# Expert layers of a graph network: the first layer's output computed transposed, four steps deep instead of six

## The reference, cut to what matters

```python
def _moe(tokens, router_w, w1, b1, w2, b2):
    logits = tokens @ router_w.T
    probs = softmax(logits)
    rw, re = top_k(probs, 2)
    rw = rw / max(rw.sum(-1), 1e-12)
    combine = zeros((N, 8)).at[arange(N)[:, None], re].set(rw)
    out = tokens
    for e in range(8):
        h = gelu(tokens @ w1[e] + b1[e])      # w1[e], w2[e]: 256 x 256
        y = h @ w2[e] + b2[e]
        out = out + combine[:, e:e + 1] * y
    return out
```

## Time and profile before

| | us |
|---|---|
| median of three runs | 2656.83 (2654.34 to 2657.34) |
| the profiled execution | 2656.25 |
| its span in the profile | 2654.4 |

### The profile page before, as it was taken

The page is one execution under the profiler, slowest core; times in us unless marked ns, Lnnn a source line. Parts: engine busy times, 40 slices in busy tenths (PEclk is TensorE's granted clock), DMA queues, the critical chain, the costliest instruction groups (busy, mean ns, idle before and its releaser), DMA issues. The chain is left out here.

```text
span 2654.4 us, 61287 instructions
## 1 busy us (share of the span) xinstructions
PE 2380.0 (90%) x15214; PEld 2044.3 (77%) x15215; DVE 2007.8 (76%) x6154; ACT 1716.5 (65%) x5986; POOL 1353.1 (51%) x1342
## 2 busy tenths in 40 slices
PE   4399999789999999999999999999999889119997
PEld 4288887568888888888888888888888779117886
DVE  8999999477777777777777777777777656546653
ACT  1777777567777777777777777777777556233432
POOL 2067777465555555555555555555555101267666
PEclk7599999989999999999999999999999989559998
DMA  7011111243232323232322332323235299156675
GB/s 151 1 34 29 34 34 29 86 114 91 87 92 87 91 87 91 87 91 87 91 87 89 89 91 87 91 87 91 87 91 86 62 289 307 67 204 203 208 123 65
DMA packets 155377, 265.16 MB, mean 100 GB/s; under 512 B 31249, under 2 KB 99440, under 8 KB 154917
## 3 DMA queue, kind: packets, MB, share of 16 engines
q0 software_dynamic: 64656, 147.39, 21.2%
q1 hardware_dynamic: 90623, 116.59, 14.6%
HBM read 190.85 MB, written 73.02 MB: 99 GB/s over the span
## 5 line engine op out<-in xcount | busy, mean ns | idle before, releaser
L1056 POOL DMA_INDIRECT work<-dst_half,stage_i x848 | 811.6, 957 | 758.3 <-PE ps L1264 582.5
L1247 PE MATMUL ps<-W2c,work 128*128 128x256 f32 x3392 | 802.3, 379 | 0.0
L1247 PEld LDWEIGHTS ps<-W2c,work 128*128 128x128 f32 x3392 | 612.0, 190 | 70.7
L1082 DVE TENSOR_TENSOR agg<-agg,ps 125x256 f32 x848 | 354.2, 418 | 254.0 <-PE ps L1264 246.3
L1188 ACT ACTIVATE work<-ps 128x512 f32<-128x512 f32 x424 | 251.9, 594 | 351.5 <-PE ps L1264 351.4
L1264 PE MATMUL ps<-work 128*125 128x256 f32 x1696 | 435.2, 379 | 1.3 <-ACT work L1209 1.3
L1203 ACT ACTIVATE work<-work 128x256 f32<-128x256 f32 x848 | 341.4, 404 | 53.6 <-DVE work L1109 50.1
L1161 DVE SCALAR_TENSOR_TENSOR work<-ps,work,b2c 128x256 f32<-128x256 f32 x848 | 368.4, 476 | 0.0
L1238 PE MATMUL ps<-ablk,work 128*128 x2544 | 351.1, 275 | 16.3 <-DVE work L1130 10.4
L519 POOL DMA_INDIRECT edge_records<-stage,work x208 | 262.6, 1263 | 176.2 <-PE ps L946 113.2
L1195 ACT ACTIVATE work<-work 128x256 f32<-128x256 f32 x848 | 340.8, 406 | 0.3
(11 more groups left out here) (280 smaller groups left out, 3366.8 us busy)
## 6 DMA issues: line engine op xcount, KB each, us to landing
work<-tile_sources SPq DMA_DIRECT2D x106, 250.0 KB
first_choice_tokens<-work SPq DMA_DIRECT2D x14, 1028.0 KB
work<-dst_half,stage_i POOLq DMA_INDIRECT x848, 2.8
second_choice_tokens<-work SPq DMA_DIRECT2D x14, 516.0 KB
work<-first_choice_tokens SPq DMA_DIRECT2D x28, 258.0 KB, 3.7
work<-second_choice_tokens SPq DMA_DIRECT2D x28, 258.0 KB, 2.9
work<-first_choice_tokens SPq DMA_DIRECT2D x28, 256.0 KB, 3.4
update_node_half<-work SPq DMA_DIRECT2D x25, 250.0 KB, 2.2
```

The lines of the kernel that those rows point to most:

```text
L1056: pool.indirect_dma_start(bg[:, r, u, :], None, dstd, bass.IndirectOffsetOnAxis(ap=stage_i[:, c:c + 1], axis=0)).then_inc(gath[r], 16)
L1082: v.tensor_tensor(d, d, ps[0:NB, (7, 0)[a.mod(2)], u * D:(u + 1) * D], ALU.add).then_inc(agg_add, 1)
L1247: last = t_.matmul(ps[:, 5 + s, u * D:(u + 1) * D], sT[:, a.mod(RT), u, k], W2c[:, k], start=(k == 0), stop=(k == KC - 1))
```

## The change

The first layer is computed with the expert's weights as the stationary operand and the transposed tokens moving, so that h comes out transposed already and the transposes of h, with ScalarE's copy of them, go. Its stationary operand is read from a fixed place: VectorE copies the two experts' `w1` of a pair to `w1p`, two pairs deep. The bias now lies along partitions, so ScalarE adds it inside the Gelu, in four activations of 128 columns per pair, and reads experts' offsets from registers of its own. `b1` is loaded as 8 rows and transposed by TensorE in the update stage instead of being broadcast by a DMA. The pipeline is four steps deep instead of six; y has four PSUM banks. The wait for `tabrow` moves from SyncE to the engines that read it.

```diff
--- before.py
+++ after.py
@@ -1293,6 +1293,7 @@
         b2b = wcut(X * D)
         rws = wcut(KC * X, "p (k e) -> p k e", k=KC)
         rwr = wcut(D)
+        b1r = wcut(D)
         ub1T = wcut(KC)
         lg = wcut(BK * X, "p (t e) -> p t e", t=BK)
         pr = wcut(BK * X, "p (t e) -> p t e", t=BK)
@@ -1353,6 +1354,7 @@
         aggcp_ready = sem("aggcp_ready")
         rw_tr = sem("rw_tr")
         rwT_ready = sem("rwT_ready")
+        b1T_ready = sem("b1T_ready")
         tb_ready = sem("tb_ready")
         tb_tr = sem("tb_tr")
         tT_ready = sem("tT_ready")
@@ -1372,11 +1374,11 @@
                 sp.dma_start(uW2s, uW2.rearrange("(k p) n -> p k n", p=P)).then_inc(uw_in, 16)
                 sp.dma_start(ub1T, ub1.rearrange("(k p) -> p k", p=P)).then_inc(uw_in, 16)
                 sp.dma_start(rwr[0:X], router_w).then_inc(uw_in, 16)
+                sp.dma_start(b1r[0:X], b1).then_inc(uw_in, 16)
                 expert_weights = [(w1s[:, 0], w1[:, 0:P, :].rearrange("e p n -> p e n")),
                                   (w1s[:, 1], w1[:, P:2 * P, :].rearrange("e p n -> p e n")),
                                   (w2s[:, 0], w2[:, 0:P, :].rearrange("e p n -> p e n")),
                                   (w2s[:, 1], w2[:, P:2 * P, :].rearrange("e p n -> p e n")),
-                                  (b1b, b1.rearrange("e n -> (e n)").partition_broadcast(P)),
                                   (b2b, b2.rearrange("e n -> (e n)").partition_broadcast(P))]
                 WAT = 2
 
@@ -1409,7 +1411,7 @@
                     step(Step(0, RP, m))
                 for n in range(NP2, 2 * UNITS):
                     empty_slots(n)
-                sp.wait_ge(fw_in, 16 * (2 * KC + 2))
+                sp.wait_ge(fw_in, 16 * (2 * KC + 1))
                 sp.wait_ge(xpads_out, 16 * (2 * UNITS + 1))
 
             @block.gpsimd
@@ -1486,9 +1488,11 @@
 
             @block.scalar
             def _(act):
-                act.wait_ge(uw_in, 64)
+                act.wait_ge(uw_in, 80)
                 act.wait_ge(rw_tr, 1)
                 nc.scalar.activation(rws, ps[:, 7, 0:KC * X].rearrange("p (k e) -> p k e", k=KC), ACT.Copy).then_inc(rwT_ready, 1)
+                nc.scalar.activation(b1b.rearrange("p (e n) -> p e n", e=X)[:, :, 0:KC],
+                                     ps[:, 7, KC * X:2 * KC * X].rearrange("p (k e) -> p e k", k=KC), ACT.Copy).then_inc(b1T_ready, 1)
 
                 def step(m):
                     if m.within(NP2):
@@ -1532,9 +1536,11 @@
             @block.tensor
             def _(pe):
                 t_ = nc.tensor
-                pe.wait_ge(uw_in, 64)
+                pe.wait_ge(uw_in, 80)
                 for k in range(KC):
-                    last = t_.transpose(ps[:, 7, k * X:(k + 1) * X], rwr[0:X, k * P:(k + 1) * P], ident[0:X, 0:X])
+                    t_.transpose(ps[:, 7, k * X:(k + 1) * X], rwr[0:X, k * P:(k + 1) * P], ident[0:X, 0:X])
+                for k in range(KC):
+                    last = t_.transpose(ps[:, 7, (KC + k) * X:(KC + k + 1) * X], b1r[0:X, k * P:(k + 1) * P], ident[0:X, 0:X])
                 last.then_inc(rw_tr, 1)
                 pe.wait_ge(rwT_ready, 1)
 
@@ -1648,7 +1654,6 @@
                 sp.wait_ge(xtab_out, 16)
                 sp.dma_start(tabrow[0:1, PADT:PADT + P],
                              xtabd.rearrange("p k -> (p k)").rearrange("(a n) -> a n", a=1)).then_inc(xtab_in, 16)
-                sp.wait_ge(xtab_in, 16)
 
             @block.vector
             def _(dve):
@@ -1741,8 +1746,8 @@
         XP = XT // 2
         XPC = XC // 2
         RX, RY, RS, RH = 8, 4, 4, 4
-        RB = 2
-        LXT, L1, LG1, L2H, LHT, L2 = 1, 2, 3, 4, 5, 6
+        RB, RW = 2, 2
+        LXT, L1, LG1, L2 = 1, 2, 3, 4
         LY = L2 + 1
         LB = RX + 2
         cut(0, restart=True)
@@ -1753,9 +1758,8 @@
         yb = cut(RY * 2 * D, "p (r u n) -> p r u n", r=RY, u=2)
         base = cut(RB * 2 * D, "p (r u n) -> p r u n", r=RB, u=2)
         xsT = cut(RH * 2 * D, "p (r n) -> p r n", r=RH)
-        hg = cut(RH * 2 * D, "p (r u n) -> p r u n", r=RH, u=2)
         hT = cut(RH * 2 * D, "p (r n) -> p r n", r=RH)
-        hb = work[:, WORK - 2 * 2 * D:WORK].rearrange("p (r u n) -> p r u n", r=2, u=2)
+        w1p = cut(RW * 2 * KC * D, "p (r u k n) -> p r u k n", r=RW, u=2, k=KC)
         w1f = w1s.rearrange("p k e n -> p k (e n)")
         w2f = w2s.rearrange("p k e n -> p k (e n)")
 
@@ -1768,10 +1772,8 @@
         xs_tr = sem("xs_tr")
         xsT_ready = sem("xsT_ready")
         slot_row = sem("slot_row")
+        w1p_ready = sem("pair_weights")
         h_ps = sem("h_ps")
-        hb_ready = sem("hb_ready")
-        hg_ready = sem("hg_ready")
-        h_tr = sem("h_tr")
         hT_ready = sem("hT_ready")
         y_ps = sem("y_ps")
         y_raw = sem("y_raw")
@@ -1853,6 +1855,7 @@
                 for t in range(BK):
                     route(t)
 
+                dve.wait_ge(xtab_in, 16)
                 regs = [v.alloc_register(f"expert_of_tile{j}") for j in range(2 * (RX + L2))]
                 offs = [None] * (2 * (RX + L2))
 
@@ -1869,14 +1872,6 @@
                         enter(m // RX)
                     for i in beside(m):
                         route(i)
-                    a = m - L1
-                    if 0 <= a < XP:
-                        dve.wait_ge(h_ps, a + 1)
-                        wait(dve, hg_ready, a - 1)
-                        for u in range(2):
-                            o = offs[2 * (b + L2 - L1) + u]
-                            last = v.tensor_tensor(hb[:, a % 2, u], ps[:, 2 + a % 2, u * D:(u + 1) * D], b1b[:, bass.ds(o, D)], ALU.add)
-                        last.then_inc(hb_ready, 1)
                     a = m - L2
                     if 0 <= a < XP:
                         r = a % RY
@@ -1884,7 +1879,7 @@
                         wait(dve, y_out[r], 32 * (a // RY))
                         for u in range(2):
                             o = offs[2 * b + u]
-                            v.tensor_tensor(yb[:, r, u], ps[:, 6 + a % 2, u * D:(u + 1) * D], b2b[:, bass.ds(o, D)], ALU.add).then_inc(y_raw, 1)
+                            v.tensor_tensor(yb[:, r, u], ps[:, 4 + a % RH, u * D:(u + 1) * D], b2b[:, bass.ds(o, D)], ALU.add).then_inc(y_raw, 1)
                         if a < XPC:
                             dve.wait_ge(base_in[a % RB], 16 * (a // RB + 1))
                         for u in range(2):
@@ -1897,6 +1892,10 @@
                         last.then_inc(yb_ready, 1)
                     a = m - LXT
                     if 0 <= a < XP:
+                        wait(dve, h_ps, a - RW + 1)
+                        for u in range(2):
+                            o = offs[2 * (b + L2 - LXT) + u]
+                            v.tensor_copy(w1p[:, a % RW, u], w1f[:, :, bass.ds(o, D)]).then_inc(w1p_ready, 1)
                         r = a % RX
                         dve.wait_ge(xs_in[r], 16 * (a // RX + 1))
                         if a >= RX:
@@ -1914,7 +1913,19 @@
                     nc.scalar.activation(ts[n_, r, XW:XB], agg[n_, t, :], ACT.Identity, bias=mv3[n_, t:t + 1, 0],
                                          scale=xscale[n_, t:t + 1]).then_inc(base_ready, 1)
 
+                act.wait_ge(xtab_in, 16)
+                regs = [nc.scalar.alloc_register(f"expert_of_tile{j}") for j in range(2 * (RX + LG1))]
+                offs = [None] * (2 * (RX + LG1))
+
+                def enter(it):
+
+                    for j in range(2 * LG1):
+                        nc.scalar.reg_mov(regs[j], 0 if isinstance(it, int) and it == 0 else regs[2 * RX + j])
+                    nc.scalar.load(regs[2 * LG1:], tabrow[0:1, bass.ds(it * (2 * RX) + PADT, 2 * RX)])
+                    offs[:] = [nc.scalar.snap(r, min_val=0, max_val=(X - 1) * D) for r in regs]
+
                 def step(m):
+                    b = m.c % RX if isinstance(m.it, int) else m.c - RX
                     a = m - LXT
                     if a.within(XP):
                         act.wait_ge(xs_tr, a.of(1, 1))
@@ -1922,19 +1933,21 @@
                         nc.scalar.activation(xsT[:, a.mod(RH)], ps[:, a.mod(2), :], ACT.Copy).then_inc(xsT_ready, 1)
                     a = m - LG1
                     if a.within(XP):
-                        act.wait_ge(hb_ready, a.of(1, 1))
-                        wait(act, h_tr, a.of(1, 1 - RH))
-                        nc.scalar.activation(hg[:, a.mod(RH)], hb[:, a.mod(2)], ACT.Gelu).then_inc(hg_ready, 1)
-                    a = m - LHT
-                    if a.within(XP):
-                        act.wait_ge(h_tr, a.of(1, 1))
+                        act.wait_ge(h_ps, a.of(1, 1))
                         wait(act, y_ps, a.of(1, 1 - RH))
-                        nc.scalar.activation(hT[:, a.mod(RH)], ps[:, 4 + a.mod(2), :], ACT.Copy).then_inc(hT_ready, 1)
-                pipeline(act, XP, L2, RX, step)
+                        for u in range(2):
+                            o = offs[2 * b + u]
```

(33 more changed lines are left out.)

## The result

The changed kernel takes 2761.74 us (2759.66 to 2763.84, 4 runs) against 2655.93 (2654.34 to 2657.34, 4 runs) in the same session: ratio 1.0396, 95% interval 1.0383 to 1.0408, some 106 us slower. The profiled execution took 2761.4 with a span of 2759.6. The prediction was 2770, range 2732 to 2832.

What follows compares the result with a forecast made beforehand. TensorE alone bounded the kernel before; the change was to make it alternate with VectorE's copies. The stage's path to 2747.8, less 3 and 2.5 at the start, plus 25 for the clock, gave 2767, so 2770 us; range 2732 to 2832.

Steps and rivals of the forecast that it cites:

- The closed ring: Last stage: second layer, y on VectorE, two copies, first layer run in turn; 6.32 then 6.05 us a pair against 4.33.
- The ring's terms: Parts of one pair's round: 0.15 to y, 1.19 or 1.46 to copies, copies 0.76, 0.24 to TensorE, layers 1.82 and 1.89.
- 2C: VectorE's two weight copies of a pair together, taken as 0.76 us, bounds 0.76 and 1.25.
- The copy: One 128x512 f32 copy within SBUF on VectorE: 0.42 us, or about 0.65 at the 400-element row's pace.
- Start: Last stage begins earlier: -3 us from SyncE not waiting for the tile table, -2.5 from the update stage.
- The update stage: Dropping the 1 MB broadcast of b1 saves 0 to 3.5 us there, taken as 2.5.
- y(0): Start of pair 0's adds on VectorE, moved from step 6 to 4: at 2399.05 in the old time.
- Clock: TensorE's clock falls in the gaps of 2.1 to 2.3 us: 25 us lost, between 0 and 48.
- the rival that took the rule for this case, 2745: Rival: the same alternation of TensorE and VectorE at full clock, 2745 us; chance 0.25.
- End: After pair 53's adds: gate work 1.28, GpSimd 0.27 later, last pairs' writes 3.72 + 3.72 + 3.4, then 8.1 us.
- The rival without a ring, 2635: Rival: copies ready before TensorE ends the second layer, only its 3.99 us a pair counts; 2635 us, chance 0.05.
- GpSimd has no say before: Before the last pairs, GpSimd's 5.1 us while routing and 3.7 later stay under 6 and do not set the pace.

Runs made afterwards that it cites:

- g1: Changed kernel with VectorE's two weight copies moved ahead of y in its step, nothing else: 2660.5 us, ratio 1.0012 to the kernel before.
- a5: Changed kernel with the copies still behind y but made one step ahead, for pair m instead of m-1: ratio 1.002 to the kernel before.
- g2: Changed kernel with each pair's weight copies made twice, the added ones into a spare buffer: 2808.7 us, ratio 1.0563 to the kernel before.
- c1: Changed kernel with the copies ahead of y and the base loads issued two pairs earlier: 2641.2 us, ratio 0.9938 to the kernel before.
- r1: The changed kernel measured again, unaltered, in another session on a second chip: 2762.3 us, ratio 1.0396 to the kernel before.
- g3: Changed kernel with each pair's token transposes done four times over, filling TensorE's gap: 2747.3 us, ratio 1.0338 to the kernel before.

## Why the prediction was right, and by how much each term was off

- *The closed ring* was the mechanism. Shown by its waits in 56 of 56 pairs, by g1 and a5, which open it in two ways and bring back nearly all, and by g2, in which a ring without a fall of the clock is longer by just the copies' time.
- *The ring's terms.* Second layer to y 0.15, y 1.19 (first half 1.46 to 1.50) and 2C = 0.76 (0.80 in some pairs) came out as written. VectorE's end to TensorE's start took 0.05, not the 0.24 of the earlier trace rows; that row is at the lower clock, but so is the first layer at 2458.09, and it starts 0.05 behind its copies as well, so what made 0.24 there stays open. The first layer took 1.89 after an idle gap, not 1.82; without one, in c1, 1.79 (2480.23 - 2478.44). Rings without a fall of the clock took 5.93 to 6.00 and 6.20 to 6.30, on average 5.95 and 6.23, for 6.05 and 6.32: 28 x 6.23 + 25 x 5.95 = 323.2 for 328.2, 5 us too much.
- *The copy.* 426 ns, taken as 420; the bound of 1.25 for two was far off. The Trainium skill, VectorE: DVE Perf Modes, section on the perf-mode tier table, gave an estimated 430 by it; the trace agrees. The 400-element copy of the earlier trace rows at 520 ns does not follow it.
- *Start.* GpSimd's memset came at 2297.68 for 2301.18: 3.5 us earlier, where 5.5 were forecast. From the table's load to the memset are now 0.7 us, which were 3.6, so the wait gave its 2.9 (forecast 3). The update stage gave about 1.4 of the 2.5: its first steps come every 6.2 us now and no longer jump, but they are still late (2152.90, 2159.21, 2165.44, 2170.54), and the table's way out and back took 7.3 us where it had taken 6.5 (2289.64 to 2296.95; before 2291.06 to 2297.55). In the experiments' traces on the two faster chips this memset comes anywhere from 2295.2 to 2300.4, so a term of 1 us here is less than that scatter. y(0) came at 2396.1, 2.6 later than forecast (2399.05 - 5.5).
- *Clock.* 343.1 us between y(0) and y(53), less 323.2 of rings, leave 19.9, where 25 were taken from bounds of 0 and 48. It is a dozen falls of 0.9 to 1.6 us on a first layer (16.8 together) and some 0.3 on the second layer behind each; in r1 ten falls leave 16.4. g3 got 15 of it back. The 25 was a guess between two rows, and that it came within 5 us is in part luck; its kind, a loss per fall of some 1.7, was right, and the frequency (about every third ring up to 2601, none from there to 2727, where most of the gaps are 1.7 instead of 2.0) wasn't to be had from the trace of before. The Trainium skill, TensorE: Matmul & The Clock Gate, section "Loop structure matters more than you think", says that a copy beside the matmuls doesn't bring the clock down, of a loop whose next matmuls follow at once. Here they do not, and the clock fell twelve times; the rival that took the rule for this case, 2745, is what g3 measures (2747) once TensorE works through most of the gap, and not what the kernel does with the gap open.
- *End.* From y(53) to the end 20.3, forecast 20.5. Gelus: four in 1.14, forecast 1.1, never in TensorE's waits. Sum of the differences: 2.6 - 5.0 - 5.1 - 0.2 = -7.7, from 2767.3 to the span of 2759.6. So rings and clock, both taken too long, made nearly all of the miss.
- *The rival without a ring, 2635.* c1 is that kernel: 2641.2, and 220.0 us between y(0) and y(53). Two things were missing from its sum: the base loads, which the ring had covered (49.7 us of waits on VectorE in g1, 19 us of time between g1 and c1), and GpSimd's 5.25 us a step while rows are routed, which the copies hand on to TensorE. (The rival's own sum has a slip: 117 - 110 is 7, not 6.) "GpSimd has no say before: 5.1 us, under 6" was right for the changed kernel and wrong for this rival.

## What to carry to other kernels

When an engine is given a new job for a partner, look at what stands ahead of it in that engine's program order: if that waits for the partner's last output, the two engines run in turns, however many buffers lie between, and the price is the sum of both parts in each round (here 5.9 to 6.3 us for 3.95). Cover is only good for the pace at which it was worked out: once a ring opens, work out each former cover again with the shorter step (here base loads, then GpSimd's writes). And a regular standstill of a matrix engine can cost more than its length, so price it, or give it work.

## What the runs showed of the hardware

- With standstills of 2.0 to 2.1 us in rounds of about 6 us the granted clock fell in about every third round (0.91 over 2400 to 2577), and the 16 matmuls behind took 3.2 to 3.7 us for 2.05. With 1.7 to 1.8 us it fell in none of the rounds of the changed kernel from 2605 to 2722. With mostly 0.4 to 0.8 us, the rest filled with transposes (g3), it stayed at 1.00 from 2400 to 2700.
- Sixteen 128 x 128 f32 products, a new weight each, take 1.79 us back to back (c1), as against 1.73 for the eight of 256 columns that they replace: here twice the weight loads cost 0.06 us in 1.73.
- One edit gave 0.9973 on one chip and 1.0012 on another, with intervals that don't touch: a ratio measured on one chip need not hold on another. Why it differs was not looked into; the kernel before took 2709 us on the first and 2657 on the other.
